# The attention loop of an adaLN block: every engine's list in another order, and the local softmax sums taken by TensorE from both halves

## The reference

```python
h = _layernorm(x, axis=-1) * (1 + ca) + sa
x = x + ga * _L0_attn_ref(h, ...)      # the part that the change touches
h = _layernorm(x, axis=-1) * (1 + cb) + sb
x = x + gb * _L0_ffn_ref(h, ...)       # unchanged
```

```python
sc = jnp.where(mask[None, None], sc, -jnp.inf)
p = jax.nn.softmax(sc, axis=-1)
out = jnp.einsum('bhnij,bhnjd->bhnid', p, Vw)
...
gl = jax.nn.sigmoid(jnp.einsum('bhsd,hd->bhs', Q, gate_local_w))[..., None]
gr = jax.nn.sigmoid(jnp.einsum('bhsd,hd->bhs', Q, gate_remote_w))[..., None]
out = gl * local + gr * rem
```

## Time and profile before

| | us |
|---|---|
| median of 3 runs | 749.49 (747.51 to 749.99) |
| profiled execution, time | 748.97 |
| its span, first to last instruction | 747.2 |
| PE busy | 645.6 |
| VectorE busy | 538.1 |
| ScalarE busy | 384.9 |
| GpSimd busy | 294.9 |

### The profile page before, as it was taken

One profiled execution on the slowest core, in us unless ns is written; L12 is line 12 of the kernel. 1 busy time (PEld: TensorE's weight loads), 2 busy tenths in 40 slices (PEclk: granted clock), 3 DMA queues, 4 the chain that ended last, 5 costly groups with the idle time before them and its releaser, 6 DMA issues.

```text
span 747.2 us, 24120 instructions
## 1 busy us (share of the span) xinstructions
PE 645.6 (86%) x8822; PEld 506.4 (68%) x8822; DVE 538.1 (72%) x1241; ACT 384.9 (52%) x910; POOL 294.9 (39%) x415
## 2 busy tenths in 40 slices
PE   5588888788888878888887888888779999999998
PEld 3366666566666656666665666666558999898996
DVE  5568788888878888887888888788755546273552
ACT  2256655666665566666555666655543223423233
POOL 2256555455555545555554555555530000000000
PEclk9699999999999999999999999999978999999999
DMA  3757111000101100010110001010140010100101
GB/s 99 174 78 96 32 24 32 21 21 21 28 22 24 31 21 21 21 28 21 24 32 21 21 21 28 21 24 18 29 44 0 10 35 15 32 24 21 34 9 49
DMA packets 65797, 24.84 MB, mean 33 GB/s; under 512 B 38440, under 2 KB 64360, under 8 KB 65648
## 3 DMA queue, kind: packets, MB, share of 16 engines
q1 hardware_dynamic: 64320, 18.25, 10.2%
q0 software_dynamic: 1456, 6.31, 5.6%
HBM read 16.13 MB, written 8.40 MB: 33 GB/s over the span
## 4 chain that ended last, share of the span: by engine, by line
PE 42%; DVE 26%; ACT 15%; issue 14%; POOL 1%; ACTq 1%; DVEq 1%; DMA 0%; SPq 0%; POOLq 0%
DVE mx L561 10%; PE SB L820 7%; PE WB L808 7%; DVE rden L634 5%; ACT PT L443 5%; PE SB L927 5%; PE WB L795 4%; PE SB L795 4%; ACT xn_d L449 4%; DVE Pr L568 3%; ACT Pr L403 3%; PE SB L882 2%; PE SB L931 2%; ACT PL L435 2%; PE WB L970 2%
## 5 line engine op out<-in xcount | busy, mean ns | idle before, releaser
L336 POOL TENSOR_TENSOR KM<-K_ch,bd_scale 128x1024 f32<-128x1024 f32 x32 | 60.6, 1893 | 125.2 <-ACT K_ch L411 125.2
L634 DVE RECIPROCAL rden<-SB 128x256 f32<-128x256 f32 x32 | 56.2, 1758 | 54.5 <-PE SB L931 54.5
L506 ACT ACTIVATE Pr<-WB,mb1T 128x256 f32<-128x256 f32 x128 | 49.8, 477 | 75.7 <-PE WB L808 75.6
L561 DVE TENSOR_REDUCE mx<-SB 128x8 f32<-128x512 f32 x128 | 87.2, 681 | 1.5 <-PE SB L882 1.5
L403 ACT ACTIVATE Pr<-Pr 128x512 f32<-128x512 f32 x128 | 80.8, 631 | 10.8 <-DVE Pr L568 7.2
L568 DVE TENSOR_TENSOR Pr<-SB,mx 128x512 f32<-128x512 f32 x128 | 84.6, 681 | 0.0
L358 POOL TENSOR_TENSOR PT_sum<-PT 128x512 f32<-128x512 f32 x64 | 80.3, 1275 | 3.8 <-ACT PT L443 3.8
L443 ACT COPY PT<-SB 128x512 f32<-128x512 f32 x128 | 66.1, 622 | 0.0
L896 PE MATMUL SB<-ident,Pr 128*128 128x128 f32 x512 | 63.0, 276 | 0.9 <-ACT Pr L403 0.9
L820 PE MATMUL SB<-Pr,GA 128*128 128x256 f32 x256 | 61.2, 381 | 0.0
L835 PE MATMUL WB<-hT,wk 128*128 128x256 f32 x64 | 23.3, 448 | 43.2 <-DVE PlB L582 43.2
(11 more groups left out here) (195 smaller groups left out, 1518.5 us busy)
## 6 DMA issues: line engine op xcount, KB each, us to landing
x_all<-in_L_attn_x SPq DMA_DIRECT2D x32, 128.0 KB, 2.1
v_rows<-V_rows SPq DMA_DIRECT2D x32, 128.0 KB, 1.8
VBD<-v_rows SPq DMA_DIRECT2D x128, 32.0 KB, 1.8
TW<-in_L_ffn_TW POOLq DMA_DIRECT2D x16, 256.0 KB, 9.5
GA<-ga_rows POOLq DMA_DIRECT2D x1, 2048.0 KB, 10.5
out_x<-attT SPq DMA_DIRECT2D x16, 128.0 KB, 1.8
out_x<-y_ga SPq DMA_DIRECT2D x16, 128.0 KB, 1.8
PT<-in_L_ffn_W SPq DMA_DIRECT2D x2, 256.0 KB
```

The source lines that it names most:

```text
L336: nc.gpsimd.tensor_tensor(KM[:, :, W:KW], bc(K_ch[:], [P, 4, S], 1), bc(bd_scale[:], [P, 4, S], 2), ALU.mult).then_inc(km_ready, 1)
L561: nc.vector.tensor_reduce(mx[:, k, :], SB[k][:].rearrange("p (h j) -> p h j", h=8), AX.X, ALU.max).then_inc(mx_ready, 1)
L634: nc.vector.reciprocal(rden[:], SB[2][:, S:2 * S]).then_inc(rden_ready, 1)
```

## The change

Four things. GpSimd's PT_sum goes; PE multiplies both halves of PT with ones_bd and lets PSUM add them, which makes eight matmuls out of four (each is two instructions in the trace). The gate matmuls read QT in place of hT, with weights that VectorE makes directly in the setup, and stand at the end of the step; a transpose, a matmul and three ScalarE copies of the setup go. Local values and denominators are written to WB2 in place of SB2, the second layer norm's hidden layer to SB0, the transposed first layer norm to SB1. And the code of `step` of all four compute engines is written in another order. What is computed stays.

The core of the diff, POOL, setup and PE:

```diff
                     pool.wait_ge(k_ready, b + 1)
                     nc.gpsimd.tensor_tensor(KM[:, :, W:KW], bc(K_ch[:], [P, 4, S], 1), bc(bd_scale[:], [P, 4, S], 2), ALU.mult
                                             ).then_inc(km_ready, 1)
-                if has(it, 0):
-                    inv_std(it, aggr_a, mv_a, ve_a, eps_a, rstd_a, rstd_a_s)
+                    pool.wait_ge(gq_ready, 2 * (b + 1))
+                    nc.gpsimd.tensor_tensor(GKBD[0:NL], bc(GKT[:], [NL, LH, NL], 1),
+                                            bc(head[0:NL, 0:LH], [NL, LH, NL], 2), ALU.mult).then_inc(gkbd_ready, 1)
...
-                if has(it, 2):
-
-                    b = it - 2
-                    both = PT[:, 0:G * 2 * S].rearrange("p (g k s) -> p g k s", g=G, k=2)
-                    for i in range(2):
-                        pool.wait_ge(pt_copied, 4 * b + 2 * (i + 1))
-                        pair = slice(2 * i, 2 * i + 2)
-                        nc.gpsimd.tensor_tensor(PT_sum[:, pair, :], both[:, pair, 0, :], both[:, pair, 1, :], ALU.add
-                                                ).then_inc(pts_ready, 1)
...
-                if has(it, 1):
-
-                    b = it - 1
-                    pool.wait_ge(gq_ready, 2 * (b + 1))
-                    nc.gpsimd.tensor_tensor(GKBD[0:NL], bc(GKT[:], [NL, LH, NL], 1),
-                                            bc(head[0:NL, 0:LH], [NL, LH, NL], 2), ALU.mult).then_inc(gkbd_ready, 1)
+                if has(it, 0):
+                    inv_std(it, aggr_a, mv_a, ve_a, eps_a, rstd_a, rstd_a_s)
...
-                    then(nc.vector.tensor_tensor(gate_cols[:, 0:2 * H].rearrange("p (k h) -> p k h", k=2), bc(head[:], [P, 2, H], 1),
-                                                 bc(gate_col[:], [P, 2, H], 2), ALU.mult))
+                    for k in range(2):
+                        beside(nc.vector.tensor_tensor(gate_w[:, k, :].rearrange("p (h d) -> p h d", d=HD), bc(head[:], [P, H, HD], 2),
+                                                       bc(gate_col[:, k:k + 1], [P, H, HD], 2), ALU.mult))
+                    dve.wait_ge(chain, n[0])
...
-                bank_free(pe, it, (0, hT_ready, 1, 1), (4, h2T_ready, 1, 1))
-                bank_free(pe, it, (4, hid_summed, 1, 1), (2, pt_copied, 4, 2))
-                bank_free(pe, it, (2, a_ready, 1, 1))
+                bank_free(pe, it, (4, h2T_ready, 1, 1), (2, pt_copied, 4, 1))
+                bank_free(pe, it, (0, hT_ready, 1, 1), (2, pt_copied, 4, 2))
+                bank_free(pe, it, (2, pt_copied, 4, 3))
...
+                pe.wait_ge(tg_ready, b + 1)
...
-                            dst = SB[2][W * g:W * g + W, kb * W:kb * W + HALF].rearrange("p (k s) -> p k s", k=2)
+                            dst = WB[2][W * g:W * g + W, kb * W:kb * W + HALF].rearrange("p (k s) -> p k s", k=2)
...
-                pe.wait_ge(pts_ready, T * (b + 1))
-                for g in range(G):
-                    last = mm(SB[2][W * g:W * g + W, S:2 * S], ones_bd[:], PT_sum[:, g, :], start=False, stop=True,
-                              skip_group_check=True)
+                for k in range(2):
+                    for g in range(G):
+                        last = mm(WB[2][W * g:W * g + W, S:2 * S], ones_bd[:], PT[:, (2 * g + k) * S:(2 * g + k + 1) * S],
+                                  start=False, stop=(k == 1), skip_group_check=True)
                 last.then_inc(pv_done, 1)
...
+            def gates(it):
+
+                bank_free(pe, it, (2, a_ready, 1, 1))
+                if isinstance(it, int) and it == 1:
+                    pe.wait_ge(ga_ready, 1)
+                for k in range(2):
+                    last = mm(WB[2][:, k * S:(k + 1) * S], gate_w[:, k, :], QT[:], start=True, stop=True)
+                last.then_inc(gates_done, 1)
+
             def latent_value_rows(it):
 
-                bank_free(pe, it, (2, lpt_copied, 2, 2), (1, gq_ready, 2, 2))
+                b = it - 1
+                pe.wait_ge(ls_sub, 2 * b + 1)
...
-            def latent_scores(it):
+            def latent_scores(it, t, m):
                 b = it - 1
-                pe.wait_ge(gq_ready, 2 * (b + 1))
-                pe.wait_ge(gkbd_ready, b + 1)
-                for t, m in ((0, W), (1, NL)):
-                    if t == 0:
-                        pe.wait_ge(gvbd_ready, b + 1)
-                    else:
-                        bank_free(pe, it, (2, remn_ready, 1, 1), (1, qt_ready, 1, 1))
-                    mm(WB[1 - t][:, 0:8 * m].rearrange("p (h j) -> p h j", h=8), GQT[:, t * P:(t + 1) * P],
-                       GKBD[:, :, 0:m], start=True, stop=True).then_inc(ls_ready, 1)
+                if t == 0:
...
+                    pe.wait_ge(gq_ready, 2 * (b + 1))
+                    pe.wait_ge(gkbd_ready, b + 1)
+                    bank_free(pe, it, (2, lpt_copied, 2, 2))
+                else:
+                    bank_free(pe, it, (2, remn_ready, 1, 1), (1, qt_ready, 1, 1))
+                mm(WB[1 - t][:, 0:8 * m].rearrange("p (h j) -> p h j", h=8), GQT[:, t * P:(t + 1) * P],
+                   GKBD[:, :, 0:m], start=True, stop=True).then_inc(ls_ready, 1)
 
             def step(it):
                 if has(it, 1):
                     projections(it)
                 if has(it, 2):
                     latent_T(it)
-                    probs_T(it)
+                    probs_T(it, 0)
+                    probs_T(it, 1)
                     latent_values(it)
                 if has(it, 1):
-                    latent_value_rows(it)
+                    latent_scores(it, 0, W)
+                if has(it, 2):
+                    probs_T(it, 2)
+                    probs_T(it, 3)
...
+                if has(it, 1):
+                    latent_scores(it, 1, NL)
                 if has(it, 4):
                     pe.wait_ge(xn_d_s, T * (it - 4 + 1))
-                    bank_free(pe, it, (2, pt_copied, 4, 1), (5, h2T_ready, 1, 1))
+                    bank_free(pe, it, (2, pt_copied, 4, 1), (5, hid_summed, 1, 1))
                     for t in range(T):
                         last = nc.tensor.transpose(SB[0][:, t * P:(t + 1) * P], xn_d[:, t, :], ident[:])
                     last.then_inc(x2T_done, 1)
+                if has(it, 0):
+
+                    pe.wait_ge(xn_a_s, T * (it + 1))
+                    bank_free(pe, it, (2, pt_copied, 4, 2), (1, hT_ready, 1, 1))
+                    for t in range(T):
+                        last = nc.tensor.transpose(SB[1][:, t * P:(t + 1) * P], xn_a[:, t, :], ident[:])
+                    last.then_inc(xT_done, 1)
+                if has(it, 1):
+                    latent_value_rows(it)
                 if has(it, 2):
                     values(it)
+                if has(it, 1):
+                    scores(it)
...
+                if has(it, 1):
+                    gates(it)
...
-                    bank_free(pe, it, (2, pt_copied, 4, 2), (5, hid_summed, 1, 1))
-                    mm(SB[1][:, 0:S], gate_w1T[:], h2T[:, bass.ds(b * S, S)], start=True, stop=True
+                    bank_free(pe, it, (1, s_sub, 4, 1))
+                    mm(SB[0][:, 0:S], gate_w1T[:], h2T[:, bass.ds(b * S, S)], start=True, stop=True
                        ).then_inc(hid_done, 1)
```

VectorE at the local softmax's end:

```diff
                     dve.wait_ge(pv_done, b + 2)
-                    nc.vector.reciprocal(rden[:], SB[2][:, S:2 * S]).then_inc(rden_ready, 1)
+                    nc.vector.reciprocal(rden[:], WB[2][:, S:2 * S]).then_inc(rden_ready, 1)
                     dve.wait_ge(rden_ready, b + 1)
-                    nc.vector.tensor_tensor(a_loc[:], SB[2][:, 0:S], rden[:], ALU.mult).then_inc(a_ready, 1)
-                if has(it, 0):
-
-                    dve.wait_ge(hT_ready, it + 1)
-                    nc.vector.tensor_reduce(hpT[:], hT[:].rearrange("p (n k) -> p n k", k=POOL), AX.X, ALU.add
-                                            ).then_inc(hp_ready, 1)
+                    nc.vector.tensor_tensor(a_loc[:], WB[2][:, 0:S], rden[:], ALU.mult).then_inc(a_ready, 1)
+                if has(it, 1):
+                    b = it - 1
+                    maximum(b, 0)
+                    lowered(b, 0)
                 if has(it, 2):
                     b = it - 2
-                    dve.wait_ge(a_ready, b + 1)
                     dve.wait_ge(tg_ready, b + 1)
+                    dve.wait_ge(rem_done, b + 1)
                     at_least(dve, att_ready, b)
-                    nc.vector.scalar_tensor_tensor(a_gated[:], tg[:, 0, :], 1.0, a_loc[:], ALU.add, ALU.mult).then_inc(ag_ready, 1)
-                    dve.wait_ge(rem_done, b + 1)
                     nc.vector.scalar_tensor_tensor(rem_g[:], tg[:, 1, :], 1.0, WB[3][:, 0:S], ALU.add, ALU.mult
                                                    ).then_inc(remg_ready, 1)
+                    dve.wait_ge(a_ready, b + 1)
+                    nc.vector.scalar_tensor_tensor(a_gated[:], tg[:, 0, :], 1.0, a_loc[:], ALU.add, ALU.mult).then_inc(ag_ready, 1)
```

(38 more changed lines are left out.)

160 lines of the change are left out of this document (75 added, 85 removed).

## The result

The changed kernel takes **707.57 us** (median of 4 runs, 707.16 to 710.46) against 749.36 (747.51 to 749.99) for the kernel before, measured beside it: a ratio of 0.9459, interval 0.9442 to 0.9476. The forecast was 700, its range 685 to 718. The profiled execution has a span of 705.8 us, 41.4 less than before.

What follows compares the result with a forecast made beforehand. In-order engines waiting on each other in a closed loop, none full, bound the 16.35 us step. Saving 1.60 x 28 = 44.8, plus 5 from filling and draining, less 0.5 setup, gives -49.3: 700 us, range 685 to 718.

Steps and rivals of the forecast that it cites:

- marks named ahead: Signs in the new step: no wait at rlden, under 0.1 at xn_a, some 0.4 at hid, denominators about 1.0 us.
- The wait at rden: VectorE's wait for the denominators, 1.75 us before, would stay at 0.7 to 1.0 us a step.
- The added matmuls: Eight more denominator matmuls on PE, taken at 0.46 us a step, bounds 0 and 1.7 us.
- inside the 0.7: PE keeps about 0.7 us of waiting a step; hid's wait for Pr0, about 0.4, was counted as idle within it.
- The loop of 14.71 through rem_n: Loop taken as longest: VectorE from denominators to rem_n 10.80, PE from second latent scores through denominators 3.91, taken as 14.75.
- PE's own list: PE's work in a step, 13.96 + 0.46 - 0.09 less modelled ends of 0.16 before two waits: 14.0 us.
- The seam of 0.09: PE's cost at a change of matmul shape; eight changes a step instead of nine would save 0.09 us.
- slow starts: PE runs a little slower after a wait, so the step was taken as 14.75 us, not 14.71.
- GpSimd's additions: Two additions, 2.51 us a step, that PE does not wait for; removing them alone would pay nothing.
- a matter of order for GKBD: Without the additions on GpSimd, GKBD can follow KM directly and the first latent scores stand earlier on PE.
- Rival 2: First latent scores wait for GKBD behind KM, with 0.1 to 0.2 us to spare; 15.3 a step, 715 us; chance 0.25.
- the filling steps: Three filling and four draining steps share part of the waits: gain between 0 and 11 us, taken as 5.

Runs made afterwards that it cites:

- e1: Kernel before, with GpSimd's two additions removed and PE summing both PT halves in sixteen matmuls, no list reordered: 762.61 us, ratio 1.0173.
- e4: Changed kernel with one more 128x512 VectorE pass, its result unused, behind Pr3 in the loop: 712.54 us, ratio 0.9506.
- e3: Changed kernel with hid moved from bank SB0 to WB1 in the loop's steps, so it no longer waits for Pr0: 696.09 us, ratio 0.9291.
- e2: Changed kernel with GpSimd's two additions and the eight denominator matmuls kept as before, additions behind the inverse deviations: 745.77 us, ratio 0.9957.
- e8: The new order with GpSimd's additions kept, plus one wait so they start only after VectorE's xn_a passes: 718.73 us, ratio 0.9579.

## Why the prediction was right, and where it was off

- **Direction and most of the marks named ahead** came as forecast: waits at rlden, xn_a and the first projection gone, 0.37 at hid (0.4 forecast), denominators 1.00 us. The wait at rden, 0.63, is a little under the 0.7 to 1.0, and the step, 14.98, a little over the 14.6 to 14.9.
- **The added matmuls:** 0.46 a step forecast; 0.45 by the rows (1.00 against 0.55), 0.43 by e1.
- **The step that failed** is the loop, and with it the sentence that hid's wait of about 0.4 is idle "inside the 0.7". The loop of 14.71 through rem_n has 0.37 us to spare, and a pass of 0.61 put into it left that path open (e4). hid's wait lies in the loop that does close, and without it the step is 0.41 shorter (e3). The followed loop was sized well: by the rows it comes to 14.66 (10.83 from the denominators' end to rem_n's, 0.05 to PE, 3.78 on PE). It is not the longest. That the time still fell into the range is in part luck: the loop that closes lies only 0.3 us a step above it.
- **The term behind that:** PE's own list. By the prediction's numbers the loop through hid was 3.7 + 14.0 - 3.3 + 0.16, about 14.55, and so shorter than 14.71. Measured it has 3.69 to Pr0's end, 0.14 from there to hid, for which the prediction has no term, and 11.15 on PE in place of 10.9.
- **What made that list longer:** put at 14.0, so that 0.7 of idle time was left, it is 14.60 less the modelled 0.16 ahead of the one wait, 14.44. Latent values and value rows take 0.21 more: 1.01 and 0.32 us apart (311.01 to 312.02, 315.27 to 315.59) where the two together had taken 1.12 (318.05 to 319.17), interleaved in part by the trace. hid takes 0.59 behind its wait, against 0.43 before and 0.44 in e3, where it waits for nothing. The gates take 0.97 against 0.87 (1.13 and 1.03 less 0.16), with no wait ahead of them; no run shows why. The seam of 0.09 that I counted as saved is not to be seen as a gain. Other blocks are shorter. For slow starts I had allowed 0.04.
- **GpSimd's additions:** that removing them alone pays nothing is right for the old order (e1). What I missed is that in the new one they would hold xn_a, or come too late (e2, e8). What I called a matter of order for GKBD is worth more: without them the new order gains 42 us, with them 3 to 31.
- **Rival 2**, a wait for GKBD, is true in steps 3 and 4 alone, 1.8 us each, since GpSimd issues the expert transfers ahead of it. That is what I left out when I took step 4 as a loop step and the filling steps as gains.
- **The sum.** Forecast 49.3, measured 41.4. 27 steady steps gave 37.3 in place of 43.2; step 4 lost 1.6 in place of gaining 1.6; setup, filling and tail gave 5.7 in place of 4.5. Together 7.9 short.

## What to carry to other kernels

When a reordering fills an engine, its small waits and slow starts behind them stop being free: write out the loop through that engine's whole list and compare it with the longest other loop before calling a wait idle. Two operations on different engines may hold each other without any semaphore, so removing one from GpSimd can be what makes a new order work. And the issue of a large transfer is an instruction in its engine's list: look at what stands behind it, and at the loop's own transfers beside it.
